# Attention and fp8 layer: input normalised in place, maxima half a batch ahead, shift rows in quarters, product with V in two steps

## What is computed

```python
xn  = layernorm(x)                                   # x: 8 batches, 512 rows, 256 columns
Q, K, V = xn @ W_q.T, xn @ W_k.T, xn @ W_v.T         # 16 heads of 16 columns; Q and K get a rotary turn
scores  = einsum('bhqd,bhkd->bhqk', Qr, Kr) * 0.25   # causal: later keys are masked
attn    = einsum('bhqk,bhkd->bhqd', softmax(scores), Vh) @ W_o.T
ffn     = fake_fp8(xn) @ fake_fp8(weight).T + bias   # scale from the largest |xn| of all batches
out     = x + attn + ffn
```

## Time and profile before

| | us |
|---|---|
| median of 3 runs (lowest, highest) | 468.45 (467.94, 469.84) |
| the profiled execution | 468.62 |
| its span, first to last instruction | 466.9 |
| PE busy | 405.5 (87%) |
| DVE busy | 350.1 (75%) |
| ACT busy | 277.3 (59%) |
| POOL busy | 274.4 (59%) |

### The profile page before, as it was taken

The page is one execution under the profiler, slowest core; times in us unless marked ns, Lnnn a source line. Parts: engine busy times, 40 slices in busy tenths (PEclk is TensorE's granted clock), DMA queues, the critical chain, the costliest instruction groups (busy, mean ns, idle before and its releaser), DMA issues.

```text
span 466.9 us, 9145 instructions
## 1 busy us (share of the span) xinstructions
PE 405.5 (87%) x2819; PEld 222.8 (48%) x2819; DVE 350.1 (75%) x1340; ACT 277.3 (59%) x500; POOL 274.4 (59%) x278
## 2 busy tenths in 40 slices
PE   1790676999889999999999999999999999998975
PEld 1440521364345556654565556555655545643443
DVE  3779899969769977997799778977897878842041
ACT  2742932147765677567666765677567656675850
POOL 2304376636746984698459844985498337226552
PEclk9996555599999999999999999999999999999999
DMA  7826747300483238422851375037504760020021
GB/s 234 257 87 197 159 136 193 81 5 18 143 214 84 69 101 204 131 69 78 216 144 46 93 213 152 32 110 206 158 18 124 194 170 2 4 93 3 1 91 46
DMA packets 37617, 53.43 MB, mean 114 GB/s; under 512 B 5152, under 2 KB 31136, under 8 KB 37536
## 3 DMA queue, kind: packets, MB, share of 16 engines
q1 hardware_dynamic: 37568, 52.84, 40.6%
HBM read 35.78 MB, written 17.04 MB: 113 GB/s over the span
## 4 chain that ended last, share of the span: by engine, by line
PE 44%; POOL 22%; ACT 11%; issue 10%; DVE 8%; DMA 3%; POOLq 1%; SPq 1%; ACTq 0%; DVEq 0%
PE st_ps L842 10%; PE o_ps L922 9%; PE s_ps L860 7%; ACT prob L722 6%; PE m_ps L894 5%; PE m_ps L869 4%; POOL prob L427 4%; POOL rot L259 4%; PE m_ps L798 4%; POOL rot L253 3%; DVE scratch L587 3%; POOL xq L457 3%; POOL parts L263 3%; POOL rot L252 2%; POOL qv L453 2%
## 5 line engine op out<-in xcount | busy, mean ns | idle before, releaser
L587 DVE CUSTOM_DVE_ANT_0 scratch<-s_ps,causal 128x512 bf16<-128x512 f32 (+3 forms) x512 | 220.9, 485 | 55.0 <-PE s_ps L860 52.9
L722 ACT ACTIVATE prob<-st_ps 128x512 f32<-128x512 f32 x320 | 174.8, 600 | 97.9 <-PE st_ps L842 97.4
L427 POOL TENSOR_SCALAR_AFFINE_SELECT prob<-prob 128x512 f32<-128x512 f32 (+1 forms) x160 | 86.4, 544 | 130.9 <-ACT prob L722 129.4
L860 PE MATMUL s_ps<-k_st,q_st 96*128 96x512 bf16 (+3 forms) x512 | 130.8, 320 | 7.0 <-DVE rowmax L587 3.2
L842 PE MATMUL st_ps<-q_st,k_st 98*128 98x128 bf16 (+3 forms) x512 | 121.9, 303 | 4.2 <-ACT prob L722 2.8
L922 PE MATMUL o_ps<-prob,v_sb 128*17 128x512 f32 (+3 forms) x1024 | 87.4, 437 | 10.0 <-ACT heads L737 5.1
L842 PEld LDWEIGHTS st_ps<-q_st,k_st 98*128 98x128 bf16 x512 | 42.0, 97 | 76.3 <-ACT prob L722 42.3
L860 PEld LDWEIGHTS s_ps<-k_st,q_st 96*128 96x128 bf16 x512 | 48.9, 99 | 43.7 <-DVE rowmax L587 20.6
L922 PEld LDWEIGHTS o_ps<-prob,v_sb 128*17 128x17 f32 x1024 | 20.5, 96 | 48.3 <-issue 36.0
L587 DVE DVE_READ_ACCUMULATOR2_ANT rowmax<- 128x1 f32 x512 | 41.7, 81 | 0.1
L894 PE MATMUL m_ps<-wo_sb,attnT 128*128 128x256 f32 x128 | 33.2, 381 | 1.8 <-DVE x_res L610 1.4
(11 more groups left out here) (99 smaller groups left out, 502.6 us busy)
## 6 DMA issues: line engine op xcount, KB each, us to landing
qk_parts<-parts SPq DMA_DIRECT2D x16, 768.0 KB, 3.7
q_st<-qk_parts SPq DMA_DIRECT2D x32, 192.0 KB, 3.3
k_st<-qk_parts SPq DMA_DIRECT2D x32, 192.0 KB, 3.7
q_st<-x_dram SPq DMA_DIRECT2D x8, 512.0 KB, 5.5
q_st<-qk_parts SPq DMA_DIRECT2D x32, 128.0 KB, 3.4
k_st<-qk_parts SPq DMA_DIRECT2D x32, 128.0 KB, 3.7
x_res<-x_dram SPq DMA_DIRECT2D x8, 512.0 KB, 3.5
out_dram<-x_res SPq DMA_DIRECT2D x8, 512.0 KB, 4.8
```

The lines of the kernel that those rows point to most:

```text
L427: eng.affine_select(out=ap, in_=ap, compare_op=ALU.is_ge, fill=0.0, base=0, pattern=pat, channel_multiplier=-1).then_inc(masked, 1)
L587: eng.tensor_tensor_reduce(scratch[:, at, col:col + w], s_ps[at][:, col:col + w], causal[:, T - w:T], 1.0, NEG, ALU.add, ALU.max, rowmax[: ...
L722: eng.activation(prob[u][:, half * T:(half + 1) * T], st_ps[ST_BANK[2 * s + half]][:, :], ACT.Exp, scale=SCALE).then_inc(exp_done, 1)
L860: mm = eng.matmul(bank[:, col:col + (qb + 1) * P], q_st[0:ROWS, 1 - par, h, qb * P:(qb + 1) * P], k_st[0:ROWS, 1 - par, h, 0:(qb + 1) * P] ...
```

## The change

One running slot number, from -10 to 175, takes the place of iterations and stages. Batch n's exponentials are in slots 20n to 20n + 19, its maxima ten slots ahead. Each small job has an offset to 20n (`OFFSETS`). Within a batch's 20 slots the jobs now stand so: V 0 and 2, mt 1, 6, 11 and 16 (the last for the next batch), o 3 to 6, at 6, 7, 9 and 11, fin 8, 10, 12 and 14, projections 10, 12, 14 and 16.

- x is loaded into `xnT` and normalised and transposed there; `prob` and `q_st` are no longer used for it. The fp8 weight is loaded into `xq`.
- The prologue projects batch 0 only. Batches 3 to 7 are normalised in slots -10 to -5, beside the maxima of batch 0; batch 1 is projected in slots -10 to -4 with the three-term product.
- `largest` is in slots 1, 3, ... 15, the weight steps in slots 16 to 21.
- Shift rows go in four quarters, one a head group.
- `pv` has two steps a head group (kb 0 in slot 5g + 3, all else in slot 5g + 6), not three (5g + 3, 5g + 5, 5g + 6).
- The quantisation of batch n starts in slot 20n + 16 (batch 0: slot 23). The last store goes in four pieces.

```diff
+OFFSETS = {("v", 0): 0, ("mt", 1): 1, ("v", 1): 2, ("o", 0): 23, ("o", 1): 24, ("o", 2): 25, ("mt", 2): 6, ("o", 3): 26,
+           ("at", 0): 26, ("at", 1): 27, ("fin", 0): 28, ("at", 2): 29, ("fin", 1): 30, ("qk", 0): -30, ("mt", 3): 11,
+           ("at", 3): 31, ("fin", 2): 32, ("qk", 1): -28, ("qk", 2): -26, ("fin", 3): 34, ("qk", 3): -24, ("mt", 0): -4}
...
+            for slot in range(FIRST_SLOT, END_SLOT):
+                for off, g in ((-3, 0), (2, 1), (7, 2), (12, 3)):
+                    n = batch_at(slot, off)
+                    if n is not None:
+                        shift_rows(n, g)
+                n = batch_at(slot, -22, 1)
+                if n is not None:
+                    query_stacks(n)
+                n = batch_at(slot, -17, 1)
+                if n is not None:
+                    key_stacks(n)
...
-                    if u == 0 and g % 2 == 0:
-                        eng.wait_ge(shift_in[g // 2], 16 * (b + 1))
+                if u == 0:
+                    c = NG * n + g
+                    eng.wait_ge(shift_in[c % 2], 16 * (c // 2 + 1))
...
-                        if s in (7, 13):
-                            low(eng, n, s // 13)
-                        if s in (3, 8):
-                            rotate(eng, n, s // 8)
-                        if s in (5, 10):
-                            remainder(eng, n, s // 10)
+                for off, step, w in ((-27, rotate, 0), (-25, remainder, 0), (-23, low, 0),
+                                     (-22, rotate, 1), (-20, remainder, 1), (-18, low, 1)):
...
-                    for kb in ((0,), (1, 3), (2,))[step]:
+                for kb, us in (((0, (0, 1)),), ((1, (2, 3)), (3, (2, 3)), (2, (4,))))[step]:
...
-                        eng.wait_ge(masked, SLOTS * bb + 5 * g + (2, 4, 5)[step])
+                    eng.wait_ge(masked, SLOTS * n + 5 * g + (2, 5)[step])
...
+                if slot in range(1, 2 * NB, 2):
+                    largest(slot // 2)
```

More of the change, by code:

```diff
@@ L61, in wait_past @@
         eng.wait_ge(sem, count)
[L64 to L68, removed]
 def unit_parts(u, half):
@@ L231, in attention_ffn_block @@
         reader = {"qk": (roped, 4), "v": (v_copied, 2), "o": (normed, 4), "at": (at_copied, 4),
[L232 to L239, removed]
+                  "fin": (fin_done, 4), "mt": (shift_done, 4)}
@@ new lines, in _ @@
+            eng.dma_start(bias_sb[:, :], bias.partition_broadcast(P)).then_inc(w_in, 16)
+            query_stacks(0)
+            key_stacks(0)
+            for slot in range(FIRST_SLOT, END_SLOT):
[9 more added lines that the diff above has]
+                    key_stacks(n)
+                n = batch_at(slot, 37 - SLOTS)
+                if n is not None and n > 0:
+                    store(n - 1)
+                n = batch_at(slot, 21)
+                if n is not None:
+                    load_residual(n)
@@ L381, in _ @@
+            store(NB - 1)
+            eng.wait_ge(y_out, 16 * (NB - 1 + NQ))
         @block.gpsimd
@@ L470, in _ @@
+            nw = NC * D
+            invert(0)
+            invert(1)
+            eng.wait_ge(ln_rstd, 4)
+            fill_ones(0)
+            eng.wait_ge(consts, 7)
+            remainder(eng, 0, 0)
+            invert(2)
+            low(eng, 0, 0)
+            split_weights(0)
+            split_weights(1)
+            split_x(1)
+            for n in range(3, 7):
+                invert(n)
             eng.memset(v_sb[:, :, :, :], 1.0).then_inc(consts, 1)
-            eng.wait_ge(consts, 7)
@@ L677, in parts_of_first @@
[L677 to L689 removed]
+                eng.wait_ge(rem_done[w], n + 1)
+                eng.copy(parts[:, w, 1], rotated_in(n, w)).then_inc(mid_done[w], 1)
@@ L974, in _, with scores @@
-            run(iteration)
+            def scores(n, s, between):
+                g, u = divmod(s, 5)
+                if u == 0:
+                    c = NG * n + g
+                    eng.wait_ge(shift_in[c % 2], 16 * (c // 2 + 1))
+                for half in range(2):
+                    i = 2 * s + half
+                    wait_past(eng, exp_done, HALVES * n + ST_BEFORE[i] + 1)
+                    for j, kb, col in unit_parts(u, half):
+                        h = g * HG + j
+                        mm = eng.matmul(st_ps[ST_BANK[i]][:, col:col + T - kb * P],
+                                        k_st[0:ROWS + SHIFT, n % 2, h, kb * P:(kb + 1) * P],
+                                        q_st[0:ROWS + SHIFT, n % 2, h, kb * P:T], start=True, stop=True)
+                    mm.then_inc(st_full, 1)
+                    if half == 0:
+                        between()
```

971 lines of the change are left out of this document (466 added, 505 removed).

## The result

The changed kernel takes 550.25 us (median of 4 runs, 549.24 to 553.06), the kernel before 468.6. The ratio is 1.175, with a 95% interval of 1.170 to 1.180. The forecast was slower at 523, with a range of 482 to 540; the direction and the place of the loss were right, the size too small.

The account below looks back on a forecast made before the run. It took TensorE to bound the middle and other engines the ends. Slot 20 at 130.3, five batches of 57.2, then 50, 38.5 and a tail of 17 gave 521.8, hence 523 us, range 482 to 540.

Parts of the forecast that it names:

- The front: Prologue up to slot 0: first maximum at 47 instead of 58.1, slot 0 at 73.5 instead of 89.6, 16 us ahead.
- Slots 0 to 19: Batch 0's slots: VectorE's added maxima and weight steps, plus a wait, make 57 us against 42.9.
- the wait at slot 10: TensorE waits for group 2's shift rows: about 5.5 us within slots 0 to 19, 8.4 in a steady batch.
- The chain to slot 10: Key write and 18 reads, then shift write and read, before TensorE may enter slot 10: 18.4 us.
- Slots 10 to 14 and the clock: Steady batch after the wait: 15.1 us of TensorE work, plus 2 for a clock fall (bounds 0 and 3).
- slot 15 to the low piece, 21.7: From TensorE's slot 15 to the keys' low piece in slot 2: GpSimd needs 21.7 us, TensorE alone 18.
- the period: Steady batch as chain 18.4, slots 10 to 14 15.1, clock 2, low piece 21.7: 57.2 us against 47.2.
- 1.8 a slot: TensorE's batch work without projections and V, 36 us spread over 20 slots, used for slots 2 to 14.
- The way from the low piece to slot 10: TensorE's work before slot 10: 12.4 us if GpSimd is on time, 10 left because the piece comes later.
- the tail: Last outputs, with the store in four pieces and the residual loaded sooner: 17 us instead of 19.5.
- Two steps of pv: Product with V in two steps a head group: costs nothing, or 1 us a batch either way.
- Rival 3: Group 2's shift-row quarter is in time at slot 10: period about 46.5, time 455 us, faster by 3%; chance 0.07.

Follow-up runs that it names:

- e1: Changed kernel with the next batch's key transfer cut in pieces in SyncE's order, most reads moved behind the shift rows; 496.63 us, ratio 1.060.
- e2: Changed kernel with the quantisation of batches 1 to 6 in slot 22 of the batch instead of slot 16; 540.45 us, ratio 1.154.
- e3: Changed kernel with the edits of e1 and e2 together; 505.27 us, ratio 1.079.
- e11: e7 with output products spread, three steps of pv and GpSimd's last quantisation step in slot 5 of the next batch; 464.06 us, ratio 0.990.
- e7: e1 with the quantisation of batches 1 to 7 starting in slot 10 of the batch instead of 16; 494.89 us, ratio 1.056.

## Why the forecast had the right sign and the wrong size

- **The front.** First maximum 47.3 (47 forecast). Slot 0 at 70.2 (73.5): from the first maximum on it took 22.9 us, of which VectorE was busy 19.6 (21.5 in the sum) and the rest was 3.3 (5.0). Slots 0 to 19 took 58.8 (57), slot 20 came at 129.0 (130.3). The total is right in part by luck: the wait at slot 10 was 9.3 us, not 5.5, and the ten slots before it took 21.0, not 24.
- **The chain to slot 10** was 18.9 us (18.4), and 18.5 to 19.6 in batches 2 to 6. Its parts in batch 2: write, landing and 18 issues 12.1 (13.2), the shift write behind the reads 5.3 (3.6), issue and landing of the last read 1.5 (1.6). Right, with an error each way.
- **Slots 10 to 14 and the clock.** 15.3 us at full clock (15.1), 17.0 to 18.1 as they ran in batches 2 to 5: 1.7 to 2.8 for the clock (2, bounds 0 to 3). Right, and the earlier trace rows was the right precedent. The clock falls a second time near slots 18 to 1 of batches 2, 3, 4 and 6 (0.88, 0.88, 0.79 and 0.79 over slots 0 to 4), which the sum did not have. It lies inside the next term and cost little: nothing in batches 2 and 3, where that way is 24.4 us as in e1 at a granted clock of 1.00, and 1.2 in batches 4 and 6.
- **The term that failed: "slot 15 to the low piece, 21.7".** It was 24.4 to 25.6 us (236.73 to 261.17 in batch 3), which is at least 2.7 of the 4.2 us by which the period was short. The prediction took the sum of GpSimd's steps, 20.2 us and 1.6 of idle at the start, as the length of the stretch, and put TensorE beside it at 18. GpSimd's work was as summed, 20.5 us, but it was idle 3.9: a second wait of 2.3 us for an exponential, whose scores stand in TensorE's queue behind a projection and a product with V. TensorE's own work was not 18 but 21.3 at full clock (e1), and it waited 2.2 for row maxima. And e2 and e3 show that GpSimd's load was the smaller part of it: with 5.5 us less of that load the way was still 22.6 at full clock and 24.1 where the clock fell, not 18. On that way GpSimd, ScalarE and TensorE wait for each other in turn.
- **The mean behind it.** "1.8 a slot" is TensorE's work spread over 20 slots. In e1 slots 5 to 9 are 2.5 a slot, of which TensorE works 2.1, and slots 15 to 19 are 2.4, of which it works 1.8 and VectorE 2.3. The way from the low piece to slot 10 was 13.1 us (199.74 to 212.80, where TensorE began to wait) and not 10, so the wait was smaller than forecast (5.8 in batch 2 instead of 8.4), and batch 1 had nearly none. This does not enter the period, which goes round by the chain: 18.9 + 18.1 + 24.4 = 61.4 instead of 57.2. The 10 does not follow from the prediction's own figures either (18 + 12.4 - 21.7 is 8.7).
- **The sum of the misses.** Slot 20 is 1.3 early, five batches are 18.4 longer, batch 6 is 3.5, batch 7 4.5 and the tail 1.7 longer: 26.8 over the 521.8 of the sum, which is the span of 548.5. The range had no case for a stretch in which engines wait for each other, nor for VectorE as the bound of light slots, though the earlier trace rows have it busy 39.3 of 47.2.
- **Two steps of pv.** "Nothing, or 1 us a batch" took nothing. It was 0.6 to 1.2 a batch.
- **Rival 3, 455 us if the quarter is in time**, was tested by e1 and is 42 us wrong. Its period, "TensorE's 45.6 plus little", is the same faulty step: the work of one engine taken as the length of the batch. Even without the late quarter the change would have lost 6%.

Of the 82 us, then, 54 are SyncE's order (the wait, and the clock that falls in it), and 28 are the balance of the table of small jobs, two steps of pv and slots 0 to 19 against the 19 gained in front. The new front itself is no loss: e11 keeps it, comes to slot 20 at 120.7 us where the kernel before does at 132.5, and is faster than both kernels, though its steady batch is still 48.0 against 47.2.

## What to carry to other kernels

A queue that only issues DMAs is an engine with an order of its own. Before a small transfer with a deadline is put behind a block of reads, add up the block's issues and the landing behind it, and cut the block at the deadline if it does not fit: here 15 reads moved were worth 54 us. Lay out work engine by engine and stretch by stretch; a mean per slot hides which engine is full there, and a job is free only beside another engine's full stretch. When a stall is removed, measure again before the next is priced: the edits of e3 and e7 freed one stretch and gave most or all of it back in the next.

## What the hardware showed that I had not expected

- A write of 8 KB to DRAM took 3.2 to 5.3 us to its semaphore behind 18 reads, 2.6 behind three (e1), and 1.35 us alone.
- One VectorE step (128x1024 f32, in place) took 2.50 us beside a GpSimd step on two inputs, and 0.69 without; the mean over eight was 1834 ns against 704. GpSimd's step and mask went from 2.13 and 0.64 to 2.56 and 1.09 in the same microseconds. e2 and e7, which move the quantisation away from GpSimd's step, bring all of these back (0.69 and 2.13). The Trainium skill (Advanced Engine Details and Errata, section on VectorE performance modes) says that VectorE's second SBUF port is shared with GpSimd, and that GpSimd instructions and VectorE instructions in a two-port mode interfere with or block each other. The traces agree in what they show; that this step ran in such a mode no run shows.
- A wait of TensorE of 4.2 to 6.5 us was each time followed by a stretch at 1.2 GHz (granted clock 0.51 from 217.5 to 224.4 in batch 2, with TensorE busy again from 218.6 on). Sixteen matmuls in the wait kept the clock at 2.4 GHz in three batches of five.
